# A one-layer vision transformer on one core: new instruction orders on all engines, two tiles' up product moved to ScalarE and GpSimd, two tiles' weighting moved to VectorE

## The reference, cut to what matters

```python
p = img2patches(x); h = layernorm(p, ln1_g, ln1_b) @ W + b; h = layernorm(h, ln2_g, ln2_b)   # 768 -> 192
q, k, v = split(layernorm(h) @ in_proj_weight.T + in_proj_bias)                              # 192 -> 3 x 192
attn = softmax(normalize(q) @ normalize(k).T * exp(min(logit_scale, log(100))))
h = h + ((attn @ v) * head_scale) @ out_w.T + out_b
up, gate = split(bitlinear(layernorm(h), w_in, g_in))                                        # 192 -> 2 x 512
h = h + bitlinear(silu(gate) * up, w_out, g_out)                                             # 512 -> 192
# bitlinear(x, w, g): y = x * rsqrt(mean(x*x) + 1e-6) * g; round(y * 127/max|y|) against round(w / mean|w|) in -1..1
```

## Time and profile before

| | us |
|---|---|
| median of 3 runs | 125.61 (125.09 to 126.04) |
| profiled execution, its own time | 125.35 |
| its span, first to last instruction | 123.5 |

### The profile page before, as it was taken

How to read it: one execution, slowest core, us unless ns; L and a number is a source line. 1 busy time by engine, 2 the same in 40 slices (tenths; PEclk the granted TensorE clock), 3 DMA queues, 4 the chain that set the end, 5 groups by cost and what they waited for, 6 DMA issues and landing times.

```text
span 123.5 us, 4889 instructions
## 1 busy us (share of the span) xinstructions
PE 114.8 (93%) x1940; PEld 95.3 (77%) x1948; DVE 104.6 (85%) x338; ACT 78.9 (64%) x179; POOL 74.6 (60%) x172
## 2 busy tenths in 40 slices
...
GB/s 90 255 194 178 182 140 163 150 180 222 310 53 0 5 0 5 5 0 5 3 5 0 5 0 5 0 5 5 0 5 3 5 0 16 47 43 53 48 50 49
DMA packets 24509, 7.68 MB, mean 62 GB/s; under 512 B 20579, under 2 KB 23909, under 8 KB 24486
## 3 DMA queue, kind: packets, MB, share of 16 engines
...
...
## 4 chain that ended last, share of the span: by engine, by line
PE 65%; POOL 10%; DVE 10%; issue 5%; ACT 5%; DVEq 0%; POOLq 0%
PE bank L750 11%; PE bank L772 8%; PE bank L773 7%; PE bank L796 6%; PE bank L784 5%; PE bank L650 4%; PE bank L654 3%; POOL yw L449 3%; PE bank L730 2%; PE bank L761 2%; PE bank L813 2%; PE bank L668 2%; PE bank L814 2%; PE bank L661 2%; PE bank L830 2%
## 5 line engine op out<-in xcount | busy, mean ns | idle before, releaser
L750 PE MATMUL bank<-w_emb_c,xT 128*128 128x192 f32 x108 | 19.3, 329 | 0.0
L654 PE MATMUL bank<-ones 128*128 128x128 f32 x126 | 19.2, 284 | 0.0
L750 PEld LDWEIGHTS bank<-w_emb_c,xT 128*128 128x128 f32 x108 | 17.3, 190 | 0.2
L654 PEld LDWEIGHTS bank<-ones 128*128 128x128 f32 x126 | 16.2, 191 | 1.0 <-issue 0.9
L381 POOL TENSOR_TENSOR rs<-mv,mhalf 128x1 f32<-128x1 f32 x9 | 5.2, 586 | 15.3 <-DVE mv L957 15.3
L772 PE MATMUL bank<-w_qkv,xhT 97*128 97x384 f32 (+1 forms) x36 | 12.0, 415 | 0.9 <-DVE qkp L1026 0.8
L773 PE MATMUL bank<-w_qkv,xhT 96*128 96x384 f32 (+1 forms) x36 | 11.7, 405 | 0.0
L449 POOL TENSOR_TENSOR yw<-yy,gout_bc 128x512 f32<-128x512 f32 x8 | 10.2, 1270 | 0.2 <-POOL yy L438 0.2
L796 PEld LDWEIGHTS bank<-vx,pT 32*32 32x32 f32 x864 | 8.5, 104 | 2.1 <-issue 1.9
L796 PE MATMUL bank<-vx,pT 32*32 32x17 f32 x864 | 9.3, 181 | 0.8 <-issue 0.8
L772 PEld LDWEIGHTS bank<-w_qkv,xhT 97*128 97x128 f32 x36 | 6.2, 189 | 4.1 <-issue 1.6
...
## 6 DMA issues: line engine op xcount, KB each, us to landing
...
```

Of the source, the lines that this page charges most:

```text
L654: nc.tensor.matmul(bank[b][:, 3 * P:4 * P], ones[:, :], ones[:, :], start=True, stop=True)
L750: mm = nc.tensor.matmul(emb_bank, xT[:, t % 3, P * k:P * (k + 1)], w_emb_c[:, 3 * (k % 2) + k // 2, :], start=(k == 0), stop=(k == KF - 1))
```

## The change

Two things are changed. First, the up product of tiles 4 and 5 goes over `upc` (ScalarE) and `yyp` (GpSimd) and no longer over `yy_` (VectorE), and the weighting of tiles 6 and 7 goes over `ywd` (VectorE) and no longer over `yw_` (GpSimd). Second, the lists of GpSimd, ScalarE, TensorE and VectorE are written anew; SyncE's list is as it was. With the lists the guarding waits change, the number of `spare` calls goes from 63 to 55 (some now into bank 1), and `tab_`, a copy of one column, moves from the end of ScalarE's list to its front. The operations themselves are the same.

```diff
-WEIGHED_ON_DVE = (8,)
-WEIGHED_ON_POOL = (0, 1, 2, 3, 4, 5, 6, 7)
-UP_COPIED = (0, 1, 2, 3)
-UP_READ = (4, 5, 6, 7, 8)
+WEIGHED_ON_DVE = (6, 7, 8)
+WEIGHED_ON_POOL = (0, 1, 2, 3, 4, 5)
+UP_COPIED = (0, 1, 2, 3, 4, 5)
+UP_READ = (6, 7, 8)
...
-            def ywd(t):
-                if t == 8:
+            def ywd(t, *freed):
+                if t == WEIGHED_ON_DVE[0]:
                     dve.wait_ge(ld_gout, 16)
...
+                wait_all(dve, freed)
                 nc.vector.tensor_tensor(out=yw[:, t % 3, :], in0=yy[:, t % 3, :], in1=gout_bc[:, :], op=ALU.mult).then_inc(ywd_ok, 1)
...
-            nv_(5); rs3_(8); e5_(0); yyp(0); yw_(0); s4_(2); s4_(3); nm3_(7); nm3_(8); an4_(2); nw_(6); nv_(6); e5_(1)
+            nv_(5); e5_(1); yyp(0); yw_(0); rs2_(8); an4_(2); f_h_(2); nw_(6); nv_(6); s4_(3); e5_(2); hg_(8); an4_(3)
...
-            yg_(8); out_(5); yy_(8); ywd(8); ax5_(8); out_(6); ri5_(8); qs5_(8); out_(7); out_(8)
+            yy_(7); ywd(6); ywd(7, (yq_ok, 5)); ax5_(6); out_(4); ri5_(6); ax5_(7); qs5_(6); ri5_(7); qs5_(7); yg_(8)
+            out_(5); yy_(8); ywd(8); ax5_(8); out_(6); ri5_(8); qs5_(8); out_(7); out_(8)
```

More of the change, by code:

```diff
@@ L1147, in _ @@
-            pT_(4); qT_(5); bst4_(3); mv4_(3); kT_(5); xc_(3); ri4_(2); ax4_(3); qs4_(2); ss_(6); ssm_(6); ng_(6); yg_(1)
-            rsum_(4); ri4_(3); np0_(6); np1_(6); np2_(6); qs4_(3); np3_(6); on_(4); qkn_(6); mx_(5); qT_(6); sm_(5); kT_(6)
-            yg_(2); pT_(5); ax5_(0); mx_(6); ri5_(0); sm_(6); rsum_(5); ss_(7); on_(5); pT_(6); ssm_(7); h2_(4); ng_(7)
-            qs5_(0); ax5_(1); bst4_(4); np0_(7); rsum_(6); mv4_(4); np1_(7); on_(6); np2_(7); xc_(4); np3_(7); ri5_(1)
-            h2_(5); ax4_(4); qkn_(7); bst4_(5); kT_(7); mv4_(5); yg_(3); ri4_(4); xc_(5); qT_(7); qs4_(4); h2_(6); ax4_(5)
@@ L1152, in _ @@
-            ax5_(2); ri4_(5); ss_(8); qs4_(5); ssm_(8); mx_(7); ng_(8); qs5_(1); ri5_(2); bst4_(6); sm_(7); np0_(8)
-            mv4_(6); np1_(8); qs5_(2); np2_(8); xc_(6); np3_(8); pT_(7); qkn_(8); ax4_(6); kT_(8); qT_(8); yg_(4); rsum_(7)
-            ri4_(6); yy_(4); qs4_(6); mx_(8); on_(7); sm_(8); ax5_(3); yg_(5); pT_(8); yy_(5); ax5_(4); h2_(7); ri5_(3)
-            out_(0); ri5_(4); bst4_(7); rsum_(8); mv4_(7); on_(8); xc_(7); qs5_(3); ax4_(7); qs5_(4); ri4_(7); yg_(6)
-            qs4_(7); yy_(6); out_(1); h2_(8); ax5_(5); bst4_(8); ri5_(5); mv4_(8); out_(2); xc_(8); qs5_(5); ax4_(8)
```

133 lines of the change are left out of this document (71 added, 62 removed).

## The result

| | before | after |
|---|---|---|
| median, us | 125.35 (124.89 to 126.04, 4 runs) | 128.03 (127.56 to 128.91, 4 runs) |
| profiled execution, us | 125.35 | 128.36 |
| its span, us | 123.5 | 126.6 |

The ratio is 1.0242, with a 95% interval of 1.0193 to 1.0291: the changed kernel is slower by 2.4%. I had forecast 126.2 and no clear change.

The account below looks back on a forecast made before the run. Bound: TensorE crowded until 72 us, with VectorE sometimes idle; then VectorE, without waits to 108. Terms: 125.35 - 1.5 (front) + 0.3 (tile 6) + 1.9 (tile 7) + 0.2 (tile 8) = 126.25, stated as 126.2; range 123.6 to 128.3 us.

Parts of the forecast that it names:

- Tile 7, +1.9: VectorE's `np0_(7)` and `np1_(7)` held under GpSimd's `yw_(1)` and `yw_(2)`: +1.9 us, bounds 0 and 2.3.
- Gain and loss together: -1.5 us: The front: slip at `qkv(0)` and VectorE idle time won between 48 and 72 us, together -1.5 us.
- The slip of 0.5 at `qkv(0)`: Front: `xhTe(0)` queued behind `xp_(3)`, which waits for pixels, delays `qkv(0)`: 0.5 us lost, bounds 0 and 1.3.
- the 2.0 gained: Front: work ahead of `emb(8)` fills VectorE's idle time between 48 and 72 us: 2.0 us won, bounds 0 and 3.67.
- Tile 6: +0.3, bounds 0 and 0.5: Behind `nv_(6)`, VectorE's fourth step may meet GpSimd's `hg_(8)`: +0.3 us.
- the rule: A VectorE instruction with two SBUF inputs meeting a wide GpSimd multiply under way waits for its end; read off `np3_`.
- Tile 5, no change: Behind `nv_(5)`, the hold of `np3_(5)` may vanish or two steps be held: 0 taken, bounds -1.1 and +1.1 us.
- Tile 8, +0.2: VectorE's steps behind `yg_(3)` should be in ahead of GpSimd's `yyp(3)`: +0.2 us, bounds 0 and 1.2.
- Tail, 0: Between `yy_(7)` and `yg_(8)`, VectorE's two `ywd` are covered by tile 8's work: 0, bounds -0.4 and +0.9 us.
- the front gains nothing: Rival: `qkv(0)`'s slip is carried along and idle time returns, 2.0 us not won: 128.2 us, chance 0.17.
- GpSimd the bound: Rival: GpSimd's late short steps in the second stage make VectorE and ScalarE wait, +1.1: 127.3 us, chance 0.12.

Follow-up runs that it names:

- e1: Kernel before, with GpSimd's wide multiply `yw_(2)` moved directly behind `nv_(7)`, three short instructions earlier: 126.27 us, ratio 1.0100.
- e2: Changed kernel, with `yw_(1)` moved behind `yyp(1)` and `yw_(2)` behind `e5_(3)` in GpSimd's list: 128.00 us, ratio 1.0225.
- e5: Changed kernel, GpSimd's list reordered around tiles 7 and 8: `yw_(1)` early, short steps up to `s4_(4)` ahead of `yw_(2)`: 127.97 us, ratio 1.0102.
- e15: Changed kernel with e3's VectorE order and a reordered GpSimd list (`yw_(1)` early, `yw_(2)` behind `s4_(4)`): 126.35 us, ratio 1.0046.
- e16: Changed kernel without `fill(5)`, two matmuls of ones (four records) ahead of TensorE's first real work: 127.40 us, ratio 1.0103.
- e8: Changed kernel with 52 small matmuls put behind `fill(0)` on TensorE, shifting every later matmul's number: 133.51 us, ratio 1.0508.
- e12: Changed kernel with the first projection early on TensorE, `sc(2)` directly behind `pv(1)`, `oTe(0)` and `h2_(0)` moved ahead: 132.73 us, ratio 1.0549.
- e4: Kernel before, with `np1_(5)` to `np3_(5)` also put ahead of `sm_(4)` on VectorE: 125.49 us, ratio 1.0023.
- e13: Changed kernel with GpSimd's `yw_` weighting only 8 of 512 columns of tile 3: 127.99 us, ratio 1.0172.
- e14: Changed kernel with VectorE's `ax5_` taking the maximum over only 8 of 512 columns of tiles 3 and 4: 131.24 us, ratio 1.0224.
- e3: As e2, and on VectorE `h_(8)` ahead of `qkn_(6)` and `np1_(5)` to `np3_(5)` ahead of `sm_(4)`: 127.43 us, ratio 1.0157.

## Why the prediction was wrong

The forecast of no clear change was wrong; the 128.03 lies within the range, near its upper end. Step by step:

- **Tile 7, +1.9: right**, in mechanism, place and size (0.94 + 0.87 = 1.81 us over the medians; e1 shows a hold of this kind at the end). That it reaches the end whole was too simple: e2 took it away and gained nothing, as the same edit opened a gap on GpSimd, and only e5 and e15, which also close that gap, came clearly below the changed kernel.
- **"Gain and loss together: -1.5 us": wrong** by 0.8 us. `qkn_(5)` came 0.7 us earlier, not 1.5. The slip of 0.5 at `qkv(0)` came, with 0.7, but was swallowed by `qkn_(1)`, the lower bound that I had given it. Of the 2.0 gained, 1.3 did not come: VectorE's idle time returned as the wait of 1.48 us for `pv(2)`. `sc(2)` stands behind `proj(0)` and `h2_(0)` and started 2.6 us later than before, and TensorE's stop of 1.16 us lay in `pv(2)`. The kernel before has such a stop too, 0.79 us in `pv(1)`; I had not looked at TensorE's "issue" time at all. How much of the 1.3 belongs to the order and how much to the stop is not settled: counted from `emb(0)`, `qkn_(4)` came 0.4 us earlier in e16 and 0.8 in e8, which is what the stop gives there, and e12, which was to price the order, priced its own faults.
- **"Tile 6: +0.3, bounds 0 and 0.5": wrong**, 1.24 us, the largest miss of a term. I counted only the four small steps (0.21 us, as taken) and overlooked `h_(8)`, which also has two SBUF inputs and which the change moved from 66 us into the reach of `yyp(1)`. I had read the rule off one kind of instruction, and it held for the others with two SBUF inputs that met a wide multiply early: `h_`, `xhd`, `ssm_`. That `h_(8)` met `yyp(1)` at all hangs on the stop in `pv(4)`, which I had not seen either.
- **Tile 5, no change: right** (1.07 us held against 1.13). e4 shows besides that this hold costs nothing at the end.
- **Tile 8, +0.2:** none; VectorE was first, as argued.
- **Tail, 0:** +0.2 between `qkn_(8)` and `out_(8)`, within the bounds.

With what was measured the sum is -0.7 + 1.2 + 1.8 + 0.2 = +2.5 of the 3.1 us of span; the other 0.6 lies between `qkn_(5)` and `qkn_(8)`, of which 0.3 is a wait of `rsum_(4)` for `pv(4)`, and the rest I cannot place. This is bookkeeping, not proof: e2 shows that a held step taken away need not come out at the end.

Of the rivals, "the front gains nothing" gave 128.2 and nearly met the time by luck, and its mark (more than 2 us idle between 48 and 72 us) was met with 2.46; but only some 0.8 of its 2.0 us came that way, the rest from `h_(8)`. "GpSimd the bound" is half true: e13 and e14 show that it does not set the end alone, and e3 beside e15 that a gap in its list costs time.
